# A graph network on one core: layer 1's destination rows handled in layer 1's own stage

## The reference, cut to what matters

```python
def _sage_mean(h, src, dst, inv_deg, W_neigh, W_self, b_self):
    neigh_sum = jax.ops.segment_sum(h[src], dst, num_segments=h.shape[0])
    h_neigh = neigh_sum * inv_deg
    return h @ W_self.T + b_self + h_neigh @ W_neigh.T
...
h = jax.nn.relu(_sage_mean(x, src, dst, inv_deg, W_neigh1, W_self1, b_self1))
h = jax.nn.relu(_sage_mean(h, src, dst, inv_deg, W_neigh2, W_self2, b_self2))
h = _sage_mean(h, src, dst, inv_deg, W_neigh3, W_self3, b_self3)
```

## Time and profile before

| | us |
|---|---|
| median of 3 runs | 5854.1 (5850.51 to 5857.34) |
| span of the profiled execution | 5848.6 |
| phase A, from the first index copy to the end of its last small store | 814 to 1350 |
| share_segments | 1350 to 1364 |
| phase B1 | 1364 to 1536 |
| phase G1 begins | 1536 |

### The profile page before, as it was taken

The page is one execution under the profiler, slowest core; times in us unless marked ns, Lnnn a source line. Parts: engine busy times, 40 slices in busy tenths (PEclk is TensorE's granted clock), DMA queues, the critical chain, the costliest instruction groups (busy, mean ns, idle before and its releaser), DMA issues. The chain is left out here.

```text
span 5848.6 us, 108545 instructions
## 1 busy us (share of the span) xinstructions
PE 4518.1 (77%) x24851; PEld 3361.7 (57%) x24851; DVE 3665.7 (63%) x13928; ACT 2790.5 (48%) x6444; POOL 3602.5 (62%) x3859
## 2 busy tenths in 40 slices
PE   3894966768998998833767747899999798776675
PEld 1573644556686687733765534566666586443674
DVE  4894855555685686844448737899999403444552
ACT  0494755553585486533221100688888423332431
POOL 0466667770372274057677860688888675777687
PEclk9997977678999999955889979999999757888897
DMA  3363546667887887955677759888888434443564
GB/s 105 119 216 103 184 150 204 207 207 237 283 292 242 288 291 241 332 163 158 204 248 164 148 93 290 250 284 284 283 284 283 152 115 139 145 146 120 130 117 65
DMA packets 726782, 1164.79 MB, mean 199 GB/s; under 512 B 104781, under 2 KB 387647, under 8 KB 726270
## 3 DMA queue, kind: packets, MB, share of 16 engines
q1 hardware_dynamic: 556220, 936.12, 49.5%
q0 software_dynamic: 134400, 161.92, 13.7%
q10 hardware_dynamic: 36000, 64.94, 3.0%
HBM read 638.98 MB, written 545.66 MB: 203 GB/s over the span
## 5 line engine op out<-in xcount | busy, mean ns | idle before, releaser
L1097 POOL DMA_INDIRECT G_V<-layer_rows,G_idx x400 | 385.0, 963 | 123.4 <-issue 111.9
L1126 PE MATMUL bank<-first_last_indicators,G_V 125*128 (+1 forms) x1600 | 270.4, 291 | 179.1 <-DVE G_V L1774 179.0
L2582 POOL TENSOR_TENSOR P_gA<-P_x,bn_scale 128x512 f32<-128x512 f32 x196 | 250.6, 1279 | 227.3 <-DMA P_x<-node_table 203.4
L1954 POOL DMA_INDIRECT out<-O_out,O_idx x200 | 318.2, 1591 | 103.0 <-issue 58.1
L1954 POOL DMA_INDIRECT node_table<-H_out,H_idx x200 | 325.5, 1627 | 90.1 <-issue 55.8
L1097 POOL DMA_INDIRECT G_x<-node_table,G_idx x200 | 191.2, 956 | 306.1 <-ACT G_idx L1083 245.4
L1126 PEld LDWEIGHTS bank<-first_last_indicators,G_V 125*128 125x128 f32 x1600 | 274.4, 259 | 183.2 <-issue 130.2
L2663 ACT ACTIVATE P_xh<-P_xh,P_nb,P_rs 128x128 f32<-128x128 f32 x784 | 320.2, 479 | 0.0
L1474 PE MATMUL bank<-B_S,B_V 127*128 127x125 f32 x2000 | 280.9, 286 | 46.9 <-DVE B_S L1450 37.3
L1474 PEld LDWEIGHTS bank<-B_S,B_V 127*128 127x128 f32 x2000 | 256.5, 200 | 59.1 <-issue 52.6
L2588 POOL TENSOR_TENSOR P_d<-P_hT,P_n 128x512 f32<-128x512 f32 x196 | 248.9, 1270 | 62.9 <-ACT P_n L2658 60.8
(11 more groups left out here) (476 smaller groups left out, 14502.4 us busy)
## 6 DMA issues: line engine op xcount, KB each, us to landing
P_x<-node_table SPq DMA_DIRECT2D x196, 512.0 KB
x_and_h<-P_xh SPq DMA_DIRECT2D x195, 512.0 KB
B_V<-values SPq DMA_DIRECT2D x250, 256.0 KB, 2.8
BN_g<-node_table SPq DMA_DIRECT2D x195, 256.0 KB
out<-P_out SPq DMA_DIRECT2D x195, 256.0 KB
node_table<-G_xg SPq DMA_DIRECT2D x97, 512.0 KB
values<-G_V SPq DMA_DIRECT2D x150, 256.0 KB
layer_rows<-A_a SPq DMA_DIRECT2D x100, 256.0 KB, 3.2
```

Source lines behind the costliest of these rows:

```text
L1097: pool.indirect_dma_start(out=rows[u][:, c, :], out_offset=None, in_=table, in_offset=bass.IndirectOffsetOnAxis(ap=idx[u][:, c:c + 1], axi ...
L1126: last = nc.tensor.matmul(m.bank[7][:, bass.ds((i * TILE + c) * 2, 2)], V[0:EP, c, :], m.ind[0:EP, bass.ds(i * TILE + c, 1), :].rearrange( ...
L1954: pool.indirect_dma_start(out=table, out_offset=bass.IndirectOffsetOnAxis(ap=idx[u][:, c:c + 1], axis=0), in_=out[u][:, c, :], in_offset=N ...
L2582: nc.gpsimd.tensor_tensor(t[v % 2][:], x[v][:, :, D:2 * D], m.Arow[:].unsqueeze(1).to_broadcast([128, TILE, D]), ALU.mult)\
```

## The change: what it does

`edges_start` handles source rows only: the destination gathers, their norm, their transposes and the two stores are gone. A new stage `first_layer` takes the place of `layer(…, 1, …)`: it gathers the destination rows, stores them raw to `XD`, normalises and turns them into `hdT`, and uses that where `layer` used the `h` loaded from `HDa`. `HDa` isn't written before layer 2. `key_row` gets a parameter `behind`, which is 1 in `first_layer`, with one bank for the key row (`bK`) and one for the turned rows (`bH`). In `edges_start` the turned sources get two banks in turn.

```diff
-        bS, bD, b1, b2, r1, r2 = m.bank[0:6]
+        bS, b1, b2, r1, r2 = m.bank[0:2], m.bank[2], m.bank[3], m.bank[4], m.bank[5]
...
-                    f.landed(s_xo, i - 4, u)
-                    gather(pool, f, idx_s, s_is, i, u, a["x"], xs_whole, s_gs)
-                    gather(pool, f, idx_d, s_id, i, u, a["x"], xd_whole, s_gd)
+                    gather(pool, f, idx, s_i, i, u, a["x"], xs_whole, s_g)
...
-                    if has(i):
-                        f.landed(s_gd, i, u, 64)
-                        sp.dma_start(edge_rows(m.XD, i), xd_whole[u][:]).then_inc(s_xo[u], 16)
-                    if has(i - 2):
-                        v = (u - 2) % 4
-                        f.after(s_hdT, i - 2)
-                        sp.dma_start(turned(m.HDa, i - 2), hdT[v][:]).then_inc(s_ho[v], 16)
                     if has(i - 4):
...
-                        f.landed(s_gs, i, u, 64)
-                        f.landed(s_gd, i, u, 64)
-                        ln.stats(dve, f, i, u, [t[u][:, c, :] for t in (xs, xd) for c in range(TILE)])
+                        f.landed(s_g, i, u, 64)
+                        ln.stats(dve, f, i, u, [xs[u][:, c, :] for c in range(TILE)])
...
-                    if has(i - 2):
-                        v = (u - 2) % 4
-                        f.after(s_T, i - 2)
-                        f.landed(s_ho, i - 6, v)
-                        nc.vector.tensor_copy(hdT[v][:], bD[:, 0:EG]).then_inc(s_hdT, 1)
...
-                        ln.relu(hs[v], [xs[v][:, c, :] for c in range(TILE)], v)
-                        ln.relu(hd[v], [xd[v][:, c, :] for c in range(TILE)], v, TILE).then_inc(s_h, 1)
+                        ln.relu(hs[v], [xs[v][:, c, :] for c in range(TILE)], v).then_inc(s_h, 1)
...
-                        f.after(s_hsT, i - 3)
-                        f.after(s_hdT, i - 3)
+                        f.after(s_hsT, i - 4)
                         first_last_sums(nc, m, hs[v], i - 2).then_inc(s_hl, 1)
                         for c in range(TILE):
-                            nc.tensor.transpose(bS[:, c * EP:(c + 1) * EP], hs[v][:, c, :], m.ident[0:EP, 0:EP])
-                            last = nc.tensor.transpose(bD[:, c * EP:(c + 1) * EP], hd[v][:, c, :], m.ident[0:EP, 0:EP])
+                            last = nc.tensor.transpose(bS[v % 2][:, c * EP:(c + 1) * EP], hs[v][:, c, :], m.ident[0:EP, 0:EP])
...
+def first_layer(nc, m, a):
+    n = m.T // TILE
+    table = m.TB1[0:m.T * 128, :]
+    with Phase(m, "B1") as P:
...
+        bA, bM, bR, bK, bH = m.bank[0:2], m.bank[2:4], m.bank[4:6], m.bank[6], m.bank[7]
+        with nc.Block() as block:
+            @block.gpsimd
+            def _(pool):
+                def body(i, u, has):
+                    f = Flow(pool, has, m)
+                    f.after(s_h, i - 4)
+                    f.landed(s_xo, i - 4, u)
+                    gather(pool, f, idx, s_i, i, u, a["x"], xd_whole, s_g)
+                sweep(pool, 0, n, n - 1, body, back=4, ahead=0, special=0)
+            @block.sync
+            def _(sp):
+                def body(i, u, has):
+                    f = Flow(sp, has)
+                    if has(i + 3):
+                        value_load(sp, m, f, i + 3, (u + 3) % 4, V, s_V, s_agg)
+                    if has(i):
+                        f.landed(s_g, i, u, 64)
+                        sp.dma_start(edge_rows(m.XD, i), xd_whole[u][:]).then_inc(s_xo[u], 16)
+                    if has(i - 4):
+                        f.after(s_r, i - 4)
+                        sp.dma_start(edge_rows(table, i - 4), rows_whole[u][:]).then_inc(s_ro[u], 16)
+                sweep(sp, -3, n, n + 3, body, back=5, ahead=3, special=0)
+                finish(sp, s_xo, n)
+                finish(sp, s_oo, n)
+                finish(sp, s_ro, n)
+            @block.vector
+            def _(dve):
+                def body(i, u, has):
+                    f = Flow(dve, has)
+                    if has(i):
+                        f.landed(s_g, i, u, 64)
+                        ln.stats(dve, f, i, u, [xd[u][:, c, :] for c in range(TILE)])
+                    if has(i - 1):
+                        ln.finish(f, i - 1, (u - 1) % 4)
+                        row_selectors(nc, m, f, i - 1, (u - 1) % 4, bK, S, s_row, s_sel, s_agg)
+                    if has(i - 4):
+                        f.after(s_T, i - 4)
+                        f.landed(s_ro, i - 8, u)
+                        nc.vector.tensor_copy(rows[u][:], bR[u % 2][0:EP, :].rearrange("p (c f) -> p c f", c=TILE)).then_inc(s_r, 1)
+                clear_pads(nc, P, dve)
+                sweep(dve, 0, n, n + 3, body, back=8, ahead=0, special=0)
+            @block.scalar
+            def _(act):
+                def body(i, u, has):
+                    f = Flow(act, has)
+                    if has(i):
+                        ln.root(f, i, u)
+                        if has(i + 4):
+                            scalar_index(nc, m.i_dst, idx, s_i, i + 4, u)
+                    if has(i - 1):
+                        v = (u - 1) % 4
+                        f.after(ln.s_nb, i - 1)
+                        f.after(s_hT, i - 5)
+                        ln.relu(hd[v], [xd[v][:, c, :] for c in range(TILE)], v).then_inc(s_h, 1)
+                    if has(i - 2):
+                        v = (u - 2) % 4
+                        f.after(s_hT, i - 2)
+                        f.after(s_m, i - 6)
+                        nc.scalar.activation(hdT[v][:], bH[:, 0:EG], ACT.Copy).then_inc(s_hdT, 1)
+                        f.after(s_agg, i - 2)
+                        nc.scalar.activation(agg[v][:], bA[v % 2][:, 0:EG], ACT.Copy).then_inc(s_ac, 1)
+                    if has(i - 3):
+                        v = (u - 3) % 4
+                        f.after(s_m, i - 3)
+                        f.after(s_T, i - 7)
+                        f.landed(s_oo, i - 7, v)
+                        nc.scalar.activation(o[v][:], bM[v % 2][:, 0:EG], ACT.Relu, bias=m.col["b1"]).then_inc(s_o, 1)
+                    if has(i - 4):
+                        Flow(act, has, m).after(s_o, i - 4)
+                        act.dma_start(turned(m.HDb, i - 4), o[u][:]).then_inc(s_oo[u], 16)
+                for g in range(4):
+                    scalar_index(nc, m.i_dst, idx, s_i, g, g)
+                sweep(act, 0, n, n + 3, body, back=8, ahead=4, special=0)
+            @block.tensor
+            def _(pe):
+                def body(i, u, has):
+                    f = Flow(pe, has)
+                    key_row(nc, m, f, i, bK, s_row, s_sel, behind=1)
+                    if has(i - 2):
+                        v = (u - 2) % 4
+                        f.after(s_h, i - 2)
+                        f.after(s_hdT, i - 3)
+                        for c in range(TILE):
+                            last = nc.tensor.transpose(bH[:, c * EP:(c + 1) * EP], hd[v][:, c, :], m.ident[0:EP, 0:EP])
+                        last.then_inc(s_hT, 1)
+                        f.after(s_ac, i - 4)
+                        add_up(nc, m, f, i - 2, v, V, S, bA[v % 2], s_V, s_sel, s_agg)
+                    if has(i - 4):
+                        f.after(s_o, i - 4)
+                        f.after(s_r, i - 6)
+                        for c in range(TILE):
+                            last = nc.tensor.transpose(bR[u % 2][0:EP, c * D:(c + 1) * D], o[u][:, c * EP:(c + 1) * EP], m.ident[:])
+                        last.then_inc(s_T, 1)
+                    if has(i - 3):
+                        v = (u - 3) % 4
+                        f.after(s_hdT, i - 3)
+                        f.after(s_ac, i - 3)
+                        f.after(s_o, i - 5)
+                        nc.tensor.matmul(bM[v % 2][:, 0:EG], m.w["self1"], hdT[v][:], start=True, stop=False)
+                        nc.tensor.matmul(bM[v % 2][:, 0:EG], m.w["neigh1"], agg[v][:], start=False, stop=True).then_inc(s_m, 1)
+                sweep(pe, 0, n, n + 3, body, back=6, ahead=0, special=0)
...
-def key_row(nc, m, f, i, bank, s_row, s_sel):
+def key_row(nc, m, f, i, bank, s_row, s_sel, behind=2):
 
 
     if f.has(i):
-        f.after(s_sel, i - 2)
+        f.after(s_sel, i - behind)
...
-        layer(nc, m, 1, m.HDa, m.HDb, m.TB1[0:m.T * 128, :])
+        first_layer(nc, m, a)
```

More of the change, by code:

```diff
@@ L1231, in edges_start @@
     with Phase(m, "A") as P:
-        idx_s, idx_d = P.slots("idx_s", [128, TILE], I32), P.slots("idx_d", [128, TILE], I32)
-        hd = P.slots("h_dst", [EP, TILE, D])
-        xs_whole, xs, xd_whole, xd = gathered(P, "x_src", "x_dst")
+        idx = P.slots("idx", [128, TILE], I32)
+        xs_whole, xs = gathered(P, "x_src")
         hs_whole, hs = edge_slots(P, "h_src")
-        hsT, hdT = P.slots("h_srcT", [128, EG]), P.slots("h_dstT", [128, EG])
-        a1T, a2T = P.slots("a1T", [128, EG]), P.slots("a2T", [128, EG])
+        hsT, a1T, a2T = P.slots("h_srcT", [128, EG]), P.slots("a1T", [128, EG]), P.slots("a2T", [128, EG])
```

(34 more changed lines are left out.)

4 lines of the change are left out of this document (1 added, 3 removed).

## The result

| | us |
|---|---|
| before, median of 4 runs | 5852.3 (5845.5 to 5857.3) |
| changed, median of 4 runs | 5780.65 (5775.5 to 5786.8) |
| ratio | 0.9874, 95% interval 0.986 to 0.9888 |
| span of the profiled execution | 5785.1 (before 5848.6) |

1.26% faster, 72 us by the medians, 63.5 us by the two profiled executions. The prediction was 5768 us, 13 us too low.

What follows compares the result with a forecast made beforehand. GpSimd's gathers were taken to bound edges_start, TensorE and DMA the old layer 1 stage, a chain of waits the new one. -246 + 160 = -86 us gave 5768 us as median, range 5728 to 5820.

Steps and rivals of the forecast that it cites:

- A: -246 us: Stage A (edges_start), losing four of eight gathers a group, falls from 536 to 290 us at 5.20 us a group.
- The circle between TensorE and ScalarE: In edges_start, a chain of waits closing every group, 5.04 us at the full clock, 8.20 at half.
- its formula: For edges_start: clock 0.96, 8% of the time at half clock, mixing 8.20 and 5.04 into 5.20 us a group.
- B1: +160 us: Stage B1 (first_layer), taking over the destination gathers, grows from 172 to 332 us at 6.25 us a group.
- The circle: In first_layer, VectorE (3.63 us) and TensorE (2.14) wait by turns: 5.77 us a round, taken as 5.85.
- The clock: TensorE's granted clock in first_layer, taken as 0.88; as rival, lower level cancels gain, 5854 or 5918 us, 14 in 100.
- the formula: For first_layer: clock 0.88, 0.24 of the time at half clock, mixing 7.99 and 5.85 into 6.25 us a group.
- Fill and drain: In first_layer, 7.0 us fill before the first statistics; at the end one last round of 6.3 and 16 drain.
- GpSimd's pace in B1: Rival: the gathers set first_layer's pace, 5.03 us a group, +102 us there, 5702 us in all; 6 in 100.
- The XD store: Rival: in first_layer the store on SP holds the gathers, 8 us more at most, 5776 us; 7 in 100.
- The count of 5.5 us a round: Round length that SP's order, load of V ahead of the store, allows in first_layer; 6.05 with longest landing.
- The prediction's weighing of rows: First_layer's clock placed between stages profiled at 0.94 and 0.71, nearer the first: 0.88.

Runs made afterwards that it cites:

- key_last: Changed kernel with the key row moved from the beginning to the end of TensorE's round in first_layer: 0.9746 of the kernel before, 5705.75 us.
- two_key_banks: Changed kernel with two banks for first_layer's key rows and one for the results, key row still first in the round: 0.9745 of the kernel before.
- rows_and_m_twice: Changed kernel with VectorE copying the results twice and TensorE making the self1 and neigh1 products twice in first_layer: 0.9884 of the kernel before.
- m_twice: Changed kernel with TensorE making each group's self1 and neigh1 products twice in first_layer, same result: 0.984 of the kernel before.

## Why the prediction was right, point by point

*A: -246 us.* Measured -246. The circle between TensorE and ScalarE was there as counted: in the middle of the stage a round takes 5.10 us where the sum was 5.04, with TensorE waiting for a2T in each.

```profile
1001.48 1.08 PE L1367 MATMUL bank<-A_a1T,weightsT 128*128 128x500 f32 x2 [1.03 <-ACT A_a2T L1353]
...
1006.58 1.08 PE L1367 MATMUL bank<-A_a1T,weightsT 128*128 128x500 f32 x2 [1.03 <-ACT A_a2T L1353]
```

The mean of 5.21, which the prediction had as 5.20, came about otherwise than its formula has it. The clock was not 0.96 throughout: it was 0.50 in the first four windows of ten us (810 to 850) and 0.70 in the fifth, the fifth and sixth steps between statistics took 7.9 and 7.4 us, and it was 0.99 in the steady part (the stage's 0.92 holds both). From the eighth group on the pace is 5.09. That the two came to the same mean is luck; the circle's length is not.

*B1: +160 us.* Measured +176. This is the term that was mis-sized, by 16 us, and it accounts for the miss of 13. Mechanism and place were right: one wait per round ahead of the key row, VectorE and TensorE by turns, and key_last, two_key_banks and rows_and_m_twice each show a side of it. Two numbers in it were off; m_twice, whose clock was 1.00, parts them:

- The circle. Its sum of 5.77 us is what the rounds written out ahead of the loop take, 5.66 to 5.78. In the loop full-clock rounds take 5.97 to 6.13, and the first one written out behind it 5.67 again. So the extra time belongs to the loop; which of its instructions take it (waits compare with registers there, and slices are computed) no run shows. The prediction bounded that part by 0.3 us, took 0.08 and should have taken nearly its upper bound. In the round of 6.15 us shown above the statistics come 0.74 after the copy and not 0.61, the aggregations 1.02 after these and not 0.89, the selectors 0.42 after the reciprocal and not 0.31. Over the stage, 49 steps of m_twice took 291.0 us, and the prediction's own at the full clock are 3 x 5.03 + 46 x 5.85 = 284.2. 7 us.
- The clock. 0.90 in the steady part, 0.88 was taken. But the mean was spent otherwise than the formula has it: in the second half of the stage the lower level fell onto TensorE's own part of every second round and not evenly over work and idle time. From 5.94, the mean with the clock at 1.00, to 6.48 is 0.54 us a group, 26.6 us in 49 steps; the formula gave 0.40 by 46, 18.4 us. 8 us.

Fill and drain, the time before the first statistics and after the last, 7.0 and 22, were 7.1 and 23.3 (1443.7 to 1467).

*The rivals.* GpSimd's pace in B1: wrong, 6.48 us and not 5.03; it came true only when the key row was moved. The XD store: the wait is there, 60 us of it, and it cost nothing, neither in the changed kernel nor after the circle was opened. The count of 5.5 us a round isn't tested by key_last's 5.07: there `add_up(i-1)`, which releases the store through the load of `V`, no longer stands behind key row i+1, and GpSimd's waits for the store were 3.1 us from 1160 to 1360 us, where the changed kernel had 40.4. The clock: a part, 20 us by the ratios of m_twice and 27 by its trace, and not enough to turn the sign. The Trainium skill's rule (TensorE: Matmul & The Clock Gate, HAM oscillation), every round beginning at the lower level, was true of 12 of 46 rounds here (their key row took 0.56 to 0.60 us and not 0.38). m_twice, which filled part of the wait with matmuls, ended it, in the direction of that section's advice to pad M. The prediction's weighing of rows came nearer than the rule.

*What would show it.* VectorE waiting for TensorE's transposes, TensorE for the selectors, 200 gathers in A, 1.26 us apart in its steady part: all seen. Of the signs of being wrong, VectorE waited for gathered rows once in B1's steady part, 1.1 us. GpSimd's idle time in B1 was larger than the 0.8 to 1.2 us a group that was named, about 1.5.

## What to carry to other kernels

When work is moved into a stage to use an idle engine, the gain is set by the order of waits in the receiving stage and not by its busy sums: here 246 us were taken out and 176 came back, of which 75 were one wait standing first in TensorE's round. So write down, for each engine, what stands behind its first wait, and look for a circle that closes within one round; either a second bank or a later place in the round opens it. Here an addition that filled TensorE's idle time made the kernel faster, and a cost added to the path looked halved. Both were TensorE's clock, and both were told from the rest by the list of round lengths, not by the mean. Such a list also shows what a stage's mean hides: A's 5.21 us a group were 5.09 and a slow start.

## What the runs showed of the hardware that was not expected

- TensorE's granted clock fell and rose by turns inside a steady stage: rounds of 5.98 and 7.6 us alternate from the stage's middle on. 1.7 us more matmul work in each round removed it, granted clock 1.00, and the kernel was 20 us faster for it.
- The same round at the full clock costs 5.66 to 5.78 us written out ahead of the loop, 5.97 to 6.13 us in it, and 5.67 us written out behind it.
- GpSimd's gathers kept 0.95 us and 0.30 of issue, whether the DMA share was 0.67 with eight in a group, 0.62, or 0.82.
